# Weights times values of two attentions on 32 by 32 parts of the array, with the values projected straight into four partition groups

## The reference, cut to what matters

```python
h = tok(x)                                     # (64, 17, 192)
# attention 0, causal
q, k, v = split(h @ W_attn + b_attn)           # each (64, 17, 12, 16)
scores = einsum('bqhd,bkhd->bhqk', q, k) / 4   # 17 x 17 for each image and head
attn = softmax(where(causal, scores, -inf))
a = einsum('bhqk,bkhd->bqhd', attn, v)         # weights times values
h = layernorm(h + a @ W_proj + b_proj)
# attention 1, without the mask, on layernorm(h); then 8 experts, the best 2 of each token
```

## Time and profile before

| | us |
|---|---|
| runs shown | 826.88, 835.30, 830.22 |
| median | 830.22 |
| the profiled execution | 831.77 |
| its span, first to last instruction | 829.96 |

### The profile page before, as it was taken

How to read it: one execution, slowest core, us unless ns; L and a number is a source line. 1 busy time by engine, 2 the same in 40 slices (tenths; PEclk the granted TensorE clock), 3 DMA queues, 4 the chain that set the end, 5 groups by cost and what they waited for, 6 DMA issues and landing times. The chain is left out here.

```text
span 830.0 us, 17940 instructions
## 1 busy us (share of the span) xinstructions
PE 715.0 (86%) x6425; PEld 623.9 (75%) x6425; DVE 533.1 (64%) x1058; ACT 443.6 (53%) x864; POOL 427.9 (52%) x375
## 2 busy tenths in 40 slices
PE   4999999999999902579898889999899988999980
PEld 4888888888888802578788778776567767999980
DVE  3788888888888711356555555588759774555543
ACT  1778878778787831334444444343264231666640
POOL 3667666666666435377777777200300022567751
PEclk9999999999999956689999999999999975999995
DMA  9855448964788449555555555310000576233324
GB/s 233 220 150 153 132 139 232 242 184 133 194 236 231 197 95 210 191 157 164 152 143 152 147 149 152 101 38 2 1 1 2 230 216 187 44 58 57 55 29 125
DMA packets 78516, 114.85 MB, mean 138 GB/s; under 512 B 8791, under 2 KB 58108, under 8 KB 78076
## 3 DMA queue, kind: packets, MB, share of 16 engines
q1 hardware_dynamic: 61246, 76.80, 33.2%
q0 software_dynamic: 14336, 35.40, 16.6%
q10 hardware_dynamic: 2880, 1.90, 0.7%
HBM read 91.83 MB, written 22.25 MB: 137 GB/s over the span
## 5 line engine op out<-in xcount | busy, mean ns | idle before, releaser
L592 PE MATMUL psum<-power,tT 128*128 128x192 f32 x864 | 160.2, 341 | 65.8 <-DVE tT L719 65.2
L592 PEld LDWEIGHTS psum<-power,tT 128*128 128x128 f32 x864 | 145.8, 197 | 77.5 <-issue 41.7
L533 POOL DMA_INDIRECT rows<-power_table,rank_row x144 | 145.5, 1010 | 66.1 <-issue 54.3
L327 PE MATMUL ps<-dft,fold 112*112 112x97 f32 x1536 | 168.0, 264 | 10.9 <-POOL fold L294 10.9
L327 PEld LDWEIGHTS ps<-dft,fold 112*112 112x112 f32 x1536 | 167.3, 180 | 11.4 <-issue 10.8
L719 DVE SCALAR_TENSOR_TENSOR tT<-rows,swaps,scaled 128x384 f32<-128x384 f32 x144 | 82.7, 616 | 119.1 <-ACT scaled L647 118.8
L647 ACT ACTIVATE scaled<-rows,swaps 128x384 f32<-128x384 f32 x144 | 80.6, 607 | 138.1 <-DMA rows<-power_table,rank_row 138.1
L301 POOL TENSOR_TENSOR ss<-uv 97x388 f32<-97x388 f32 x96 | 82.2, 877 | 97.1 <-ACT uv L367 97.1
L399 DVE TENSOR_TENSOR folded<-ps,far 112x388 f32<-112x388 f32 x192 | 98.4, 553 | 46.7 <-ACT far L355 46.5
L294 POOL TENSOR_TENSOR fold<-img 112x896 f32<-112x896 f32 x48 | 103.4, 2154 | 14.8 <-DMA img<-in_x 8.7
L416 DVE TENSOR_TENSOR uv<-ps,odd 97x388 f32<-97x388 f32 x192 | 97.7, 549 | 2.6 <-ACT odd L360 2.6
(11 more groups left out here) (174 smaller groups left out, 933.9 us busy)
## 6 DMA issues: line engine op xcount, KB each, us to landing
img<-in_x SPq DMA_DIRECT2D x48, 784.0 KB, 5.2
power_table<-power SPq DMA_DIRECT2D x16, 576.0 KB
power<-in_w_tok SPq DMA_DIRECT2D x3, 1728.0 KB, 10.2
power<-in_w SPq DMA_DIRECT2D x8, 579.0 KB, 7.6
power<-in_w SPq DMA_DIRECT2D x4, 1152.0 KB, 10.8
rows<-power_table,rank_row POOLq DMA_INDIRECT x144, 3.1
power_table<-power SPq DMA_DIRECT2D x1, 1200.0 KB
power_table<-power SPq DMA_DIRECT2D x1, 1072.0 KB, 15.1
```

What stands on the lines that cost most here:

```text
L327: last = pe.matmul(ps1[0:HALF, j % 2, i, col:col + FREQ], fold[:, j // UPG % FOLD_RING, part, x0:x0 + HALF], dft[:, part * FREQ:(part + 1) ...
L533: pool.indirect_dma_start(out=rows[:, j % RING, half, :], out_offset=None, in_=table[0:RECORDS if j % CHUNKS < PLAIN else RECORDS + P * (L ...
L592: last = pe.matmul(ps[:, q % 2, 0:DIM], points[:, j % SWAPPED, c, s].rearrange("p h b -> p (h b)"), wt[:, c, s, chunk, :], start=(chunk == ...
```

## The change

`own_values`, `place_v` and the constants `spread` and `own_v` are gone. `project_v` now writes each image's values to four partition groups: head h goes to group h mod 4, three heads to a group, 48 columns for an image. The host reorders the columns of the value weights to that. This takes 64 products of 32 by 48 in place of 4 of 128 by 192, on four column parts of the array. The scores are kept 32 apart instead of 17 (`LANE`), with zeros in the gap that GpSimd sets once at the end of the gathers (`padded`), so that `p_transposes` turns four heads at a time: 6 transposes instead of 4, 768 columns instead of 512, in banks 1 and 2. `values` becomes 96 products of 17 rows, 32 by 16, each on its own 32 by 32 part: row group i is the head's group, column group r the image; the four row groups write to banks 4 to 7. `share_out` reads those four banks. In TensorE's order values now comes before p_transposes. The output projections rotate over three banks instead of four, and at step 9 one of them is done instead of four. The busy work that ends attention 0 waits for the last `share_out`.

```diff
@@ -39,6 +39,9 @@
 LANES = 4
 LANE = P // LANES
 HS = HPH * SEQ
+HSETS = HEADS // LANES
+V_COLS = HSETS * HEAD
+TURNS = 2 * HSETS
 SCALE = HEAD ** -0.5
 EXPERTS, HIDDEN, TOPK = 8, 768, 2
...
@@ -538,6 +539,8 @@
         for n in range(STEPS):
             step(n, n)
+        pool.wait_ge(points_used, STEPS)
+        pool.memset(W["s"][:, :, :, SEQ:LANE], 0.0).then_inc(W["padded"], 1)
     def by_position(buf, first, count):
...
@@ -777,15 +780,13 @@
 def attention_buffers(sb, space):
-    sizes = [AUNITS // 2 * UI * DIM, 2 * 2 * DIM, 4 * 2 * HEADS * SEQ, 2 * LANES * P, 2 * 2 * DIM]
-    at = [sum(sizes[:n]) for n in range(6)]
-    v_half = lambda buf: buf.rearrange("p (u r g e) -> p u r g e", u=AUNITS // 2, g=2, r=LANES)
+    sizes = [AUNITS * UI * V_COLS, 4 * 2 * HEADS * LANE, 2 * TURNS * P, 2 * 2 * DIM]
+    at = [sum(sizes[:n]) for n in range(5)]
     return {
-        "v_own": [v_half(space[0:HS, at[0]:at[1]]), v_half(sb("v_own", [HS, sizes[0]])[:])],
-        "v": space[:, at[1]:at[2]].rearrange("p (r n) -> p r n", r=2),
-        "s": space[:, at[2]:at[3]].rearrange("p (r h t) -> p r h t", r=4, t=SEQ),
-        "pT": space[0:HS, at[3]:at[4]].rearrange("p (r n) -> p r n", r=2),
-        "o": space[:, at[4]:at[5]].rearrange("p (r h d) -> p r h d", r=2, d=HEAD),
+        "v": space[:, at[0]:at[1]].rearrange("p (u n e) -> p u n e", u=AUNITS, n=UI),
+        "s": space[:, at[1]:at[2]].rearrange("p (r h t) -> p r h t", r=4, t=LANE),
+        "pT": space[:, at[2]:at[3]].rearrange("p (r m n) -> p r m n", r=2, n=P),
+        "o": space[:, at[3]:at[4]].rearrange("p (r h d) -> p r h d", r=2, d=HEAD),
         "mx": sb("mx", [P, AUNITS, 2 * HEADS]),
         "rs": sb("rs", [P, AUNITS, 2 * HEADS]),
...
@@ -839,13 +840,13 @@
     G = AUNITS
-    SCORE_BANK, TURN_BANK, VALUE_BANK, V_BANK, BACK_BANK, OWN_BANK = 0, 1, 2, 3, 3, 4
-    X_BANK, QK_BANK, OUT_BANK = 4, (6, 7, 1, 2), 4
+    SCORE_BANK, TURN_BANK, V_BANK, BACK_BANK, VALUE_BANK = 0, 1, 3, 3, 4
+    X_BANK, QK_BANK, OUT_BANKS, BACK_TURN_BANK, SPARE_BANK = 4, (6, 7, 1, 2), (0, 1, 2), 4, 7
     raw_in = [S(f"raw_in{c}") for c in range(NC)] if not L1 else None
     x_tr, xT_done, qk_mm, q_act, k_dve, k_act = [S(n) if L1 else None for n in (
         "x_tr", "xT", "qk_mm", "q_act", "k_dve", "k_act")]
-    v_mm, v_out, own_mm, v_done = S("v_mm"), S("v_out"), S("own_mm"), S("v_done")
+    v_mm, v_out, padded = S("v_mm"), S("v_out"), W["padded"]
     t_tr, tT_done, twice = [S(n) if L1 else None for n in ("t_tr", "tT", "twice")]
     stat0, pow0 = [S(n) if not L1 else None for n in ("stat0", "pow0")]
...
@@ -889,7 +890,7 @@
                 if lag <= t < G + lag:
                     f(t - lag)
             if tile_part and t >= G + 1:
-                while tiles < TT and (t == G + 3 or (output_units(tiles) <= t - 4 and (t > G + 1 or tiles < 4))):
+                while tiles < TT and (t == G + 3 or (output_units(tiles) <= t - 4 and (t > G + 1 or tiles < 1))):
                     tile_part(tiles)
                     tiles += 1
@@ -963,24 +964,15 @@
                 pe.wait_ge(xT_done, 2 * min(NC, -(-(u + 1) * UT // TC)))
             at_least(pe, v_out, u)
             at_least(pe, oT_done, u - 4)
-            for g in range(2):
+            for n in range(UI):
+                first = (u * UI + n) * LANE
                 for h in range(2):
                     rows = KH if L1 else KH + h
-                    first = image(u, g, 0) * LANE
-                    last = pe.matmul(psum[:, V_BANK, g * DIM:(g + 1) * DIM], xT[0:rows, h, first:first + P],
-                                     W["wv"][0:rows, h, :], start=(h == 0), stop=(h == 1))
+                    for i in range(LANES):
+                        last = pe.matmul(psum[i * LANE:(i + 1) * LANE, V_BANK, n * V_COLS:(n + 1) * V_COLS],
+                                         xT[0:rows, h, first:first + LANE],
+                                         W["wv"][0:rows, h, i * V_COLS:(i + 1) * V_COLS], start=(h == 0), stop=(h == 1))
             last.then_inc(v_mm, 1)
-
-        def own_values(u):
-            if L1 and u == 0:
-                qk_complete(pe)
-            pe.wait_ge(v_out, u + 1)
-            at_least(pe, v_done, u)
-            for r in range(LANES):
-                lane = slice(r * LANE, r * LANE + SEQ)
-                last = pe.matmul(psum[0:HS, OWN_BANK + r, 0:2 * DIM], W["spread"][lane, :], v[lane, u % 2, :],
-                                 start=True, stop=True)
-            last.then_inc(own_mm, 1)
         def scores(u):
...
@@ -1002,22 +994,27 @@
         def p_transposes(u):
             pe.wait_ge(exped, u + 1)
             at_least(pe, pT_done, u)
-            for n in range(LANES):
-                last = pe.transpose(psum[0:HS, TURN_BANK, n * P:(n + 1) * P],
-                                    s[:, u % 4, n * HPH:(n + 1) * HPH, :].rearrange("p h t -> p (h t)"), W["identity"])
+            if u == 0:
+                pe.wait_ge(padded, 1)
+                if L1:
+                    qk_complete(pe)
+            for n in range(TURNS):
+                last = pe.transpose(psum[:, TURN_BANK + n // LANES, n % LANES * P:(n % LANES + 1) * P],
+                                    s[:, u % 4, n * LANES:(n + 1) * LANES, :].rearrange("p h t -> p (h t)"), W["identity"])
             last.then_inc(p_tr, 1)
         def values(u):
-            pe.wait_ge(v_done, u + 1)
             pe.wait_ge(pT_done, u + 1)
+            pe.wait_ge(v_out, u + 1)
             at_least(pe, o_done, u)
-            for g in range(2):
-                for h in range(2):
+            for m in range(TURNS):
+                g, hh = m // HSETS, m % HSETS
+                for i in range(LANES):
+                    keys = slice(i * LANE, i * LANE + SEQ)
                     for r in range(LANES):
-                        at = (g * 2 + h) * P + r * LANE
-                        last = pe.matmul(psum[r * LANE:(r + 1) * LANE, VALUE_BANK, (g * 2 + h) * KH:(g * 2 + h + 1) * KH],
-                                         pT[:, u % 2, at:at + LANE],
-                                         v_own[u // (G // 2)][:, u % (G // 2), r, g, h * KH:(h + 1) * KH], start=True, stop=True)
+                        last = pe.matmul(psum[r * LANE:(r + 1) * LANE, VALUE_BANK + i, m * HEAD:(m + 1) * HEAD],
+                                         pT[keys, u % 2, m, r * LANE:(r + 1) * LANE],
+                                         v[keys, u, g * LANES + r, hh * HEAD:(hh + 1) * HEAD], start=True, stop=True)
             last.then_inc(av, 1)
         def o_transposes(u):
@@ -1033,12 +1030,14 @@
         def out_projection(t):
             if t == 0:
                 pe.wait_ge(W["pads_set"], 17)
-                pe.wait_ge(v_done, G)
+                pe.wait_ge(less, G)
+            if t == 1:
+                pe.wait_ge(pT_done, G)
             pe.wait_ge(oT_done, output_units(t))
-            at_least(pe, z_done, t - 3)
+            at_least(pe, z_done, t - 2)
             for h in range(2):
-                last = pe.matmul(psum[:, OUT_BANK + t % 4, 0:DIM], xT[0:KH + h, h, t * P:(t + 1) * P],
+                last = pe.matmul(psum[:, OUT_BANKS[t % 3], 0:DIM], xT[0:KH + h, h, t * P:(t + 1) * P],
                                  W["wp"][0:KH + h, h, :], start=(h == 0), stop=(h == 1))
             last.then_inc(proj, 1)
...
@@ -1069,7 +1068,7 @@
         else:
             pe.wait_ge(W["pads_set"], 17)
             qk_complete(pe)
-        by_units([(1, scores), (0, project_v), (1, own_values), (2, p_transposes), (3, values), (4, o_transposes)],
+        by_units([(1, scores), (0, project_v), (3, values), (2, p_transposes), (4, o_transposes)],
                  out_projection)
         if L1:
             pe.wait_ge(less, G)
@@ -1077,13 +1076,13 @@
             pe.wait_ge(pT_done, G)
             for c in range(NC + 1):
                 if c < NC:
-                    busy_work(pe, W, psum[:, VALUE_BANK + 1, :], (1, 2, 0)[c])
+                    busy_work(pe, W, psum[:, SPARE_BANK, :], (1, 2, 0)[c])
                     t_transposes(c)
                 if c >= 1:
                     router_logits(c - 1)
         else:
-            pe.wait_ge(less, G)
-            busy_work(pe, W, psum[:, SCORE_BANK, :], 7)
+            pe.wait_ge(o_done, G)
+            busy_work(pe, W, psum[:, SPARE_BANK, :], 7)
     def program_scalar(act):
         act.wait_ge(W["in"], W["in_n"])
@@ -1116,17 +1115,19 @@
         def copy_v(u):
             act.wait_ge(v_mm, u + 1)
-            at_least(act, own_mm, u - 1)
-            act.activation(v[:, u % 2, :], psum[:, V_BANK, 0:2 * DIM], ACT.Copy).then_inc(v_out, 1)
+            act.activation(v[:, u], psum[:, V_BANK, 0:UI * V_COLS].rearrange("p (n e) -> p n e", n=UI), ACT.Copy
+                           ).then_inc(v_out, 1)
         def exponent(u):
             act.wait_ge(less, u + 1)
-            act.activation(s[:, u % 4], s[:, u % 4], ACT.Exp, scale=SCALE).then_inc(exped, 1)
```

(44 more changed lines are left out.)

21 lines of the change are left out of this document (8 added, 13 removed).

## The result

The changed kernel takes 926.87 us in the median (925.08 to 931.68), against 831.16 us for the kernel before on the same chip (826.88 to 835.30). The ratio is 1.116, with a 95% interval of 1.109 to 1.123. The prediction was 823 us, with 850 as its upper end. Ratios are of fast executions alone; one of the twelve of a later run (values first, with late projections) took 2518.80 us and is left out.

What follows compares the result with a forecast made beforehand. TensorE's steps were taken to bound the attentions at 5.12 us a unit, falling to 4.91. Gains of 2.2 + 1.3 = 3.5 us per attention, 7.0 for two, gave 831.77 - 7.0 = 824.8, or 823.2 as median; range 814 to 850.

Steps and rivals of the forecast that it cites:

- rival C: Instruction supply in the attentions: packets fetched only one after another, 9.0 us a unit, 873 us (848 half hidden); chance 0.08.
- The sign that the prediction gave for it: TensorE from 538 to 588 us: idle time that nobody releases would show that instruction supply binds.
- The four starts in 0.03 us: Start of old `values`: four matmuls and five loads begun between 560.77 and 560.80, read as 7.5 ns a pair.
- rival B: Middling pace in `values`: row groups' loads follow each other, 8 to 12 ns a pair, 830 to 843 us; chance 0.10.
- A's 20 ns: Floor for each record in `values` and `project_v`: about 20 ns wherever it goes, 885 us; chance 0.08.
- TensorE's sum for a unit: TensorE's steps in an attention unit: 0.70 + 1.50 + 1.20 + 0.64 + 0.57 = 4.61 us, against 5.12 before.
- the ring through bank 3: project_v waits for copy_oT on bank 3: project_v, values, p_transposes, copy_pT, copy_oT and semaphores make the period 4.91 us.
- my own formula: Price of pace in `values`: each 1 ns more costs 0.19 us in about 7.5 units, 3 us in all.
- The clock (D): Clock falls inside the attentions: 837 us if in every second unit, 850 if in every unit; chance 0.10.
- No wait for `padded`: GpSimd's fill at the end of the gathers, about 3.5 us, delays nobody; otherwise 2 us at most.
- The end of an attention: Last scores to first residual add: 9.0 us instead of 11.29, 2.2 less, 0.9 given back by later projections.

Runs made afterwards that it cites:

- the loop of two turns: Changed kernel with each unit's `values` products done twice, in a hardware loop of 2 over the same instructions: 963.22 us.
- the filler: Changed kernel with three products of 512 columns in front of each unit's `values`: 936.62 us, 9.8 above the changed kernel's median.
- the looped block: Kernel before with 768 small products behind attention 0's busy work, as 16 turns of a hardware loop over 48: 849.33 us, 12.3 more.
- The straight block: Kernel before with 768 small products (17 rows, 32 by 16) written out behind attention 0's busy work: 878.47 us, 41.4 more.

## Why the prediction was wrong

**The step that failed** is the one on instruction supply, in rival C: "A packet takes about 1.07 us by itself ... and would be hidden". The transfer was read rightly (1.05 us here) and taken for the price. When one packet is needed after the other they start 3.3 to 4.4 us apart, 3.76 in the mean. The period forecast for a unit, 4.91 us, was less than half of the 10.6 us that 362 / 128 = 2.83 packets take so; 10.98 were measured in the unit shown. The sign that the prediction gave for it, idle time of TensorE that nobody releases, is what the trace shows. Rival C had the mechanism, the count (2.9 packets a unit) and the condition, with a chance of 0.08. Its size was short in two terms: 3.1 us a packet, taken from small data loads, where it is 3.76, which makes 10.6 instead of 9.0 us a unit; and "the first two units covered by what is already in", where TensorE stalls for 2.22 us up to 548.44, in project_v of the second unit, after the attention's first 215 pairs. With 3.76 and seven units C's own sum would have been (10.6 - 4.9) x 7 = 40 per attention and 823 + 80 = 903 us, against 927 measured; what is left over is not taken apart here, but for the long stall of attention 1. The rows to weigh it were at hand: the densest unit of the kernel before asks for 88 pairs in 5.12 us, 7.4 us a packet, so nothing in those rows could show that faster than that is free.

Here the Trainium skill was given too much weight. Its page "Runtime: NRT & Kernel Launch", section Instruction fetch mechanics, says that instructions come in blocks of 16 KiB, 256 of them, and that fetching them is mostly hidden, because dispatch is the slower side. The size of the blocks this trace bears out to the instruction. Hidden they are not, by the rows, once 256 instructions take TensorE less than some 3.8 us.

**Pace.** In attention 1 one `values` ran without a stall:

```profile
749.28 1.85 PE L1015 MATMUL psum<-power 17*32 17x16 f32 x192
```

Less 0.25 us for the last record's own length that is 8.3 ns a record, at a clock of 0.89, and 112 records in 1.13 us at full clock give 7.9. I took 5.5, between 4 and 7.5. The four starts in 0.03 us, 7.5 ns a pair, were close to the truth. The step from there to 4 ns was a misreading: it has seven pairs passed by then, where the rows count four matmuls and five loads. So rival B had the right pace, and A's 20 ns is out (rows above, and the loop of two turns). "TensorEngine Tiling (Array Packing)", Instruction Overhead, in the Trainium skill has about 60 cycles of overhead a matmul, by an estimate 25 ns at 2.4 GHz. Between records on sixteen parts the rows show a third of that. With 7.9 to 8.3 ns TensorE's sum for a unit would be 4.61 + 192 x 2.4 to 2.8 ns, 5.1 us, and the ring through bank 3, which has values in it too, 4.91 + 0.5 = 5.4. A unit would take no less than before (5.12), so even with instructions at no cost the change would have gained at most at the ends of the attentions: 830 to 832 us by my own formula, no change. This is worked out, not run.

**The clock (D)** fell as feared, for 52.8 and 61.4 us of the two attentions, and hid behind the supply, as the filler shows. So long at half clock was not among D's prices. Whether the clock would fall as far with instructions at no cost, no run shows for the whole kernel; the looped block shows only that it can fall without stalls.

**What held.** project_v's 128 records of 48 columns at 10 ns: 113 in 1.42 us. copy_pT 0.81 us for 768 columns (0.80 taken). share_out over four banks 0.56 us, no longer than before. No wait for `padded` or for VectorE in front of TensorE's steps. The end of an attention: projections moved behind the last values gained 2.0 us in attention 1 and 3.7 us or so in all, as a term of its own in the kernel before; I had 1.3 per attention. A slip of 0.1 us in my sum there (11.29 less 9.0 is 2.3, not 2.2) changes nothing. The ring through bank 3 (4.91 us) was never reached.

**When the next packet starts.** The straight block lets the 3.8 us be taken apart. Its second packet starts at 603.34 us: the 128 records before it ended at 603.10, and the first record behind it starts at 605.67. So 2.3 us go from the start of the packet to its first record and 1.43 us into the records, with next to nothing in parallel. It is so in all eleven stalls of the block: the packet starts between 0.4 us before and 0.25 us behind the end of the records before it, and TensorE resumes 2.2 to 2.7 us later. Where the records are slower than that, as in the changed kernel between its stalls, a packet starts while TensorE still works, but never less than 3.3 us behind the one before.

**Left open.** Why 2.3 us pass from a packet's start to its first record, with 1.05 us of transfer, and why the next isn't asked for earlier, no run shows. The changed kernel with its `values` once in a loop, or with the loads of `in_w` moved away from attention 1, wasn't run.

## What to carry to other kernels

Count TensorE's instructions, not only its columns. In these kernels an unrolled stream got 128 load and matmul pairs in 3.3 to 4.4 us, about 29 ns a pair, so a stretch that needs the next 128 sooner stalls, whatever the array could do. float32 doubles the count. Where a trace shows TensorE idle with no releaser, see whether the records between two such gaps are a multiple of 128. If they are, fewer and larger products help (22 us less in attention 0 for 96 pairs less a unit), work that fills the gaps is cheap (25.0 us of it cost 7.0), and a faster array doesn't help; a loop ran the same products in 19 us instead of 43, but only as a block by itself. Before splitting a product over parts of the array, divide the new count of pairs by 128 and set some 3.8 us against each.

## What the runs showed that was not expected

- Supply works as a gate and not as a rate: 128 pairs in 1.43 us, then 2.0 to 2.6 us of standing still, in which the next packet is fetched. The lead that was built up before is small and gone after one burst: 209 pairs in the straight block, behind 14 long records, and 215 at the start of attention 0.
- A loop takes its instructions from what is already there: 1,440 records with one packet. But its turns aren't hidden behind the next packet (3.4 to 6.7 us from start to start in the kernel with two turns).
- While other loads took 86% of the DMA engines' time, the instruction packets started 6.4 us apart and one stall took 5.33 us.
- Small products on sixteen parts don't hold the full clock: in the loop the granted clock was 0.50 from 598.70 us on, with TensorE busy 12.74 of 13.70 us. Three products of 512 columns per unit brought the mean of a stretch from 0.65 to 0.99.
